# Two of seven panels of a propagation body summed from rows fetched by index instead of from the dense adjacency

## The reference

```
row, col = edge_index                      # src, dst
deg_row, deg_col = number of edges by row and by col, at least 1
w = rsqrt(deg_row[row] * deg_col[col])
def spmm(feat): return segment_sum(feat[col] * w[:, None], row, num_segments=n)
out = h
for _ in range(10):
    out = spmm(out) * 0.9 + h * 0.1
return out / theta
```

## Time and profile before

| | us |
|---|---|
| median of 2 runs | 3998.53 |
| lowest and highest | 3998.01, 3999.06 |
| the profiled execution, its span | 3998.4 |
| TensorE busy | 3854.9 |
| VectorE busy | 1769.7 |
| ScalarE busy | 1314.9 |
| GpSimd busy | 586.7 |

### The profile page before, as it was taken

The page is one execution under the profiler, slowest core; times in us unless marked ns, Lnnn a source line. Parts: engine busy times, 40 slices in busy tenths (PEclk is TensorE's granted clock), DMA queues, the critical chain, the costliest instruction groups (busy, mean ns, idle before and its releaser), DMA issues.

```text
span 3998.4 us, 124106 instructions
## 1 busy us (share of the span) xinstructions
PE 3854.9 (96%) x46183; PEld 3660.9 (92%) x46183; DVE 1769.7 (44%) x4393; ACT 1314.9 (33%) x3901; POOL 586.7 (15%) x714
## 2 busy tenths in 40 slices
PE   3889999999989999999999999999999998999999
PEld 2679999999956667999999999999999998999999
DVE  8999999999973324222222222222222222331111
ACT  1248888888871111222222122222222221111110
POOL 1016666666630000000000000000000000000000
PEclk9989999999989999999999999999999999999999
DMA  1039999889963333665665665656656665667775
GB/s 41 3 79 235 232 238 233 233 235 237 231 189 111 111 111 111 220 202 202 205 204 201 203 204 203 200 203 205 201 201 204 204 200 177 202 219 213 209 214 156
DMA packets 438001, 747.73 MB, mean 187 GB/s; under 512 B 197331, under 2 KB 330579, under 8 KB 437840
## 3 DMA queue, kind: packets, MB, share of 16 engines
q1 hardware_dynamic: 433346, 744.61, 61.1%
q10 hardware_dynamic: 4494, 0.77, 0.1%
HBM read 621.82 MB, written 83.32 MB: 176 GB/s over the span
## 4 chain that ended last, share of the span: by engine, by line
PE 91%; DVE 6%; ACT 1%; issue 1%; DMA 0%; ACTq 0%; DVEq 0%; SPq 0%; POOL 0%; POOLq 0%
PE sum L1795 49%; PE sum L1443 19%; PE pk L1182 10%; PE pr L1205 7%; PE pq L1194 3%; PE pc L1218 2%; DVE onerank L799 2%; PE l L475 1%; DVE bt L771 1%; DVE prodb L788 1%; DVE vals L781 1%; PE l L459 0%; DMA X<-in_x_dram 0%; DVE H L283 0%; PE sum L1622 0%
## 5 line engine op out<-in xcount | busy, mean ns | idle before, releaser
L1795 PE MATMUL sum<-u2b,ring 128*128 128x192 f16 x12005 | 994.1, 246 | 0.0
L1795 PEld LDWEIGHTS sum<-u2b,ring 128*128 128x128 fp8e4 x12005 | 993.1, 98 | 0.3
L1795 PE MATMUL sum<-y,ring 128*128 128x192 f16 x11662 | 962.9, 246 | 0.0
L1795 PEld LDWEIGHTS sum<-y,ring 128*128 128x128 fp8e4 x11662 | 962.2, 98 | 0.0
L1804 DVE TENSOR_TENSOR z<-lo,sum 128x96 f32<-128x96 f32 x441 | 112.2, 254 | 983.1 <-ACT lo L1819 982.8
L1182 PE MATMUL pk<-kv,hT 128*128 128x192 f16 x4900 | 485.6, 246 | 2.0 <-DVE hT L1074 2.0
L1443 PE MATMUL sum<-u,ring 128*128 128x385 f16 x2401 | 404.6, 329 | 12.4 <-ACT u L1585 12.4
L1182 PEld LDWEIGHTS pk<-kv,hT 128*128 128x128 f16 x4900 | 409.9, 99 | 2.4 <-DVE hT L1074 2.3
L1443 PEld LDWEIGHTS sum<-u,ring 128*128 128x128 fp8e4 x2401 | 236.0, 98 | 174.2 <-issue 13.6
L1264 ACT ACTIVATE kvs<-pk 128x384 f32<-128x384 f32 x735 | 301.0, 437 | 112.5 <-PE pk L1182 92.0
L1819 ACT ACTIVATE lo<-sum 128x96 f32<-128x96 f32 x441 | 110.1, 250 | 649.3 <-PE sum L1795 648.9
(11 more groups left out here) (254 smaller groups left out, 3363.3 us busy)
## 6 DMA issues: line engine op xcount, KB each, us to landing
ring<-adjacency_t SPq DMA_DIRECT2D x490, 800.0 KB, 4.3
ring<-adjacency SPq DMA_DIRECT2D x147, 896.0 KB, 4.9
rows<-slot_rows_d SPq DMA_DIRECT2D x249, 320.0 KB, 4.0
adjacency<-row SPq DMA_DIRECT2D x49, 800.0 KB, 4.4
adjacency_t<-col SPq DMA_DIRECT2D x49, 800.0 KB, 4.6
col<-row SPq DMA_TRANSPOSE x245, 4.1
out_dram<-X SPq DMA_DIRECT2D x6, 336.0 KB
slot_rows_d<-T SPq DMA_DIRECT2D x2, 240.0 KB
```

The source lines that it names most:

```text
L1795: m = pe.matmul(ps[r][:, 0:2 * D], w[:, t // 2, :, t % 2], n["this"][:, t, 0:2 * D], start=t == 0, stop=t == TILES - 1)
```

## The change

In steps 1 to 9 (nine of ten) panels 5 and 6 of each body are no longer read from the dense transpose. For each of the 25 lists of such a tile, GpSimd issues an indirect DMA (`gathers`): it takes 128 row numbers from a column of `k.index` and fetches those rows of 384 bytes from a copy of the table in memory (`u_d`) into `got[h][:, g, :]`. TensorE then sums 25 matmuls, with a 128x128 one-hot matrix of the list as weights (which slot belongs to which of the 128 nodes) and the fetched rows. There are two buffers `got`, and with two panels per body the first always serves panel 5 and the second panel 6: a panel's gathers wait until the same panel's matmuls of the body before are done. At a step's first body they also wait until the whole table is in memory (`k.u_out`); SyncE stores it body by body (`publish`), each store behind the loads of the next body.

The one-hot matrices of the 14 picked tiles are made once, by VectorE in the softmax layer (`one_hots`, seven ahead of the sums of block 0 and seven ahead of those of block 1, two buffers, each rewritten when its store has landed), and stored by GpSimd (`store`); SyncE loads them (400 KB) in place of those panels. The row numbers are computed once by GpSimd (`indices`) from the slots, which SyncE now copies to memory ahead of the attention's loads and GpSimd reads back with eight strided loads. The loops over bodies are written out inside the loop over pairs of steps on TensorE, SyncE and GpSimd. Several semaphores are used a second time instead of new ones.

```diff
+PICKS = 2
+PICKED = RING - PICKS
+PICKED_TILES = BODIES * PICKS
...
+    def sync():
+        sp.dma_start(k.slots_d, k.slots[:].rearrange("p i t g -> p (i t g)")).then_inc(k.slots_kept.sem, 16)
+        paired(sp, sync_step, SP_LAG)
...
+class Picked:
...
+    def indices(self):
...
+                pool.dma_start(planes[:, i, j * BODIES:(j + 1) * BODIES, :],
+                               of[:, i, PICKED + j:TILES:RING, :]).then_inc(k.slots_back.sem, 16)
...
+        pool.tensor_copy(k.index[:], part[1][:]).then_inc(k.listed.sem, 1)
+
+    def one_hots(self, j):
+        k, v = self.k, self.k.v
+        v.wait_ge(k.listed.sem, k.listed.at(2))
+        for b in range(j * BODIES, (j + 1) * BODIES):
+            if b >= 2:
+                v.wait_ge(k.hot_out[b % 2].sem, k.hot_out[b % 2].at(16 * (b // 2)))
+            v.tensor_tensor(self.hots[b % 2][:], under(k.count1[:], GROUPS), over(self.which[:, b, :], P),
+                            ALU.is_equal).then_inc(k.hot_built.sem, 1)
+
+    def store(self):
+        k, pool = self.k, self.k.pool
+        for b in range(PICKED_TILES):
+            pool.wait_ge(k.hot_built.sem, k.hot_built.at(b + 1))
+            pool.dma_start(k.hots_d[b, :, :], flat(self.hots[b % 2][:])).then_inc(k.hot_out[b % 2].sem, 16)
...
+            picked.one_hots(0)
             for i in range(BODIES):
+                if 1 <= i < PICKS:
+                    picked.one_hots(i)
                 v.wait_ge(k.agg.sem, k.agg.at(i))
...
         scalar(), vector(), scalar_sums(), tensor(), blocks.sync(early=1), first_loads()
+        picked.indices(), picked.store(), picked.end()
...
+    got = [k.buf(ctx, f"got{i}", [P, GROUPS, 2 * D], F16) for i in range(2)]
...
-            sp.dma_start(k.ring[r][:, 0:WIDE], k.t_d[RING * n["body"] + r, :, :]).then_inc(k.ring_in[r].sem, 16)
+            if r >= PICKED and n["turn"]:
+                sp.dma_start(k.ring[r][:, 0:GROUPS * P], k.hots_d[(r - PICKED) * BODIES + n["body"], :, :]).then_inc(k.ring_in[r].sem, 16)
+            else:
+                sp.dma_start(k.ring[r][:, 0:WIDE], k.t_d[RING * n["body"] + r, :, :]).then_inc(k.ring_in[r].sem, 16)
+
+    def publish(at, rows_of, h, b):
+
+        sp.wait_ge(k.u_ready.sem, k.u_ready.at(TILES + RING * at + RING))
+        k.settle(sp)
+        sp.dma_start(k.u_d[h][RING * b * P:RING * (b + 1) * P, :].rearrange("(t p) d -> p t d", p=P),
+                     rows_of[:, tiles_of(b), 0:2 * D]).then_inc(k.u_out[h].sem, 16)
+
+    def gathers(n):
+
+        b = n["body"]
+        if b == 0:
+            pool.wait_ge(k.u_out[n["table"]].sem, k.u_out[n["table"]].at(16 * BODIES * n["times"]))
+        for j in range(PICKS):
+            h, at = (PICKS * n["turn"][0] + j) % 2, j * BODIES + b
+            pool.wait_ge(k.done.sem, k.done.at(RING * (n["at"] - 2 // PICKS) + PICKED + j + 1))
+            k.settle(pool)
+            for g in range(GROUPS):
+                pool.indirect_dma_start(got[h][:, g, :], None, k.u_d[n["table"]], bass.IndirectOffsetOnAxis(
+                    ap=k.index[:, at, g:g + 1], axis=0)).then_inc(k.got[h].sem, 16)
...
+            if r >= PICKED and n["turn"]:
+                turn, seen = PICKS * n["turn"][0] + r - PICKED, PICKS * n["turn"][1]
+                pe.wait_ge(k.got[turn % 2].sem, k.got[turn % 2].at(16 * GROUPS * (seen + turn // 2 + 1)))
+                k.settle(pe)
+                w = k.ring[r][:, 0:GROUPS * P].bitcast(F8).rearrange("p (g e) -> p g e", e=P)
+                for g in range(GROUPS):
+                    m = pe.matmul(ps[r][:, 0:2 * D], w[:, g, :], got[turn % 2][:, g, :],
+                                  start=g == 0, stop=g == GROUPS - 1)
+                m.then_inc(k.done.sem, 1)
+                continue
```

More of the change, by code:

```diff
@@ L1850, in last_products, with sync, publish_before, gpsimd @@
                 unit.sums()
+    def sync():
+        for b in range(1, BODIES):
+            loads({"body": b, "at": b, "turn": None})
+            publish(b - 1, Ub, 1, b - 1)
+        with sp.Fori(0, last // 2) as s:
+            for n in pair(s):
+                loads(n)
+                publish_before(n)
+        for n in last_each():
+            loads(n)
+            if n["body"] == 0:
+                publish_before(n)
+    def publish_before(n):
+        h, b = n["table"], n["body"]
+        if b == 0:
+            publish(n["at"] - 1, n["this"], h, BODIES - 1)
+        else:
+            publish(n["at"] - 1, Ua if n["this"] is Ub else Ub, 1 - h, b - 1)
+    def gpsimd():
+        with pool.Fori(0, last // 2) as s:
+            for n in pair(s):
+                gathers(n)
+        for n in last_each():
+            gathers(n)
     def last_rows():
-        for n in last_numbers():
+        for n in last_each():
             b = n["body"]
@@ L1896, in last_copies @@
                 unit.root()
-    for n in numbers(sp):
-        loads(n)
-    for n in numbers(pe):
-        products(n)
+    sync(), tensor(), gpsimd()
     for n in numbers(v):
@@ L1905, in appnp_and_convolutions @@
         copies(n)
-    for n in last_numbers():
-        loads(n)
-    last_products(), last_rows(), last_copies()
+    last_rows(), last_copies()
     of_all = STEPS * BODIES
```

96 lines of the change are left out of this document (77 added, 19 removed).

## The result

The changed kernel takes 7825.85 us (median of 2 runs, 7824.85 to 7826.86) against 3998.53: 1.957 times as long (95% interval 1.953 to 1.961). The forecast was slower, and it was; but it said 5714 us with a range of 4600 to 6950, and the measured time lies 2112 us above the one and 876 above the other. The profiled execution has a span of 7821.8 us.

The account below looks back on a forecast made before the run. Matmuls bound the kernel before; GpSimd's gather issue would bind after. 3346 us of gathers plus 110 for steps, minus 1797, plus 54 preparation and 3 copy, gave +1716 on 3998.4: 5714 us, range 4600 to 6950.

Parts of the forecast that it names:

- TensorE's pace: Steps 1 to 9: matmuls bound the stretch before; 48 fewer per body save 4.0 us, 251 us over 63 bodies.
- The gather's price: GpSimd's issue of each gather: 1.06 us, ends 0.33 and 1.7; 3150 gathers make 3346 us in place of 1797.
- The overlap: Each body: panels 0 to 4 take 20.4 us beside the gathers, so the 50 issues alone set 53 us.
- The steps' gaps: Start of each step: first gather waits for the whole table, a 12.2 us chain; 110 us in sum.
- The transfers: DMA in each body: ring loads, gathers and publishing take 25 us, under the body's 53, so cost nothing.
- The preparation: Softmax layer: one-hot comparisons and indices make TensorE wait 31 and 23 us, 54 together, between 10 and 100.
- VectorE holds GpSimd back: Rival, in each body: descriptors stop for VectorE's two-input operations, 256 us more, 5970 us; chance 0.2, within the likeliest case.
- One gather at a time: Rival, GpSimd's queue: each gather waits for the landing before it, 1.7 us each, 7723 us; chance 0.05.
- Issue is hidden: Rival, GpSimd's queue: gathers under 0.52 us hide under TensorE, body 24.5 us, 3804 us; chance 0.03.
- the gather's spacing: Sign in the profile after, on GpSimd: one gather per about 1.06 us.
- the DMA share: Sign in the profile after, in the steps: DMA share near 0.45.
- TensorE's wait ahead of each picked panel ended by the gathers: Sign in the profile after, at panels 5 and 6: TensorE waits before each until its gathers end the wait.

Follow-up runs that it names:

- B: Series on chip 13, changed kernel with one edit each: plain loads by SyncE 4385 us; 64 rows a gather 7848; 32 bytes a row 7828; contiguous rows 7827.
- E: Series on chip 7 again: the changed kernel unedited, 7827 us; the changed kernel with TensorE's and GpSimd's code looped by turns, step 9 written out, 7825 us.
- F: Series on chip 10, one kernel: the changed kernel with 16-row gathers in odd steps, full gathers in even steps, 26 gathers a body in step 9; 7596 us.
- A: Series on chip 7, changed kernel with one edit each: no gathers 3808.8 us; plain loads by GpSimd 4183; 16 rows a gather 5994; TensorE's code looped 6310.
- C: Series on chip 4, edits of the changed kernel: 32 rows a gather 6060 us; 26 gathers a body, code written out 4430, TensorE's code looped 4433.
- D: Series on chip 15, changed kernel with one edit each: 26 gathers (first lists) 4433 us; 38 gathers 5357; 48 rows a gather 6110; GpSimd's code looped 6313.

## Why the forecast was wrong

The miss is 2112 us. By the forecast's terms, against the kernel with TensorE's loop (6307.7 us of span, held nowhere) and the changed kernel. The last column takes the gathers' price and the steps' gaps from the kernel at full pitch; what is left of its 5583 us is put down to the hold. The steps of the former, in the same columns as above:

```profile
1802.00:5875.00 4073.00, 1799.61 (x18679) 1737.25 (x18677) 406.47 (x1354) 347.62 (x1255) 2991.61 (x3150) 0.71 0.43 120
```

| term | forecast | full pitch | the change |
|---|---|---|---|
| 3150 gathers | 3346 | 3150 x 1.25 = 3938 | 3938 |
| steps' starts and ends | 110 | 4073 - 3938 = 135 | 135 |
| TensorE held beside them | 0 | 0 | 5583 - 4073 = 1510 |
| preparation, copy of the slots | 57 | 38 | 38 |

**TensorE's pace.** That the stretch was bound by matmuls before the change is right: without the gathers it gave what 48 matmuls a body are worth.

**The gather's price, mis-sized.** I took 1.06 us from the edge loads, since each reads its address from on-chip memory; it is 1.25 us, inside my ends of 0.33 and 1.7. This is worth 592 us. The likeness was luck: 0.53 us of the price are there with a plain load of as many rows too, the other 0.72 only with the indirect form, and of the whole only 0.10 go with 112 of the rows. The 0.62 us of the Trainium skill ("SBUF — State Buffer", section "SBUF: two separate sides") is the time of one GpSimd DMA alone and not of its issue; a plain issue takes 0.53 us here, a gather twice the page's figure.

**The overlap, the step that failed.** The prediction has it that "panels 0 to 4 (245 matmuls) take 20.4 us at the full clock, and panel 5 is done long before t = 53". In the changed kernel they take 85 us, because TensorE does not run at its pitch beside the gathers. I had looked for what could hold GpSimd back and never for what GpSimd could hold back. With it the body is 70.4 + 15.5 (the 168 matmuls left) + 3.0 (the first picked panel, which frees its buffer) = 88.9 us, and gathers and matmuls add where they should have overlapped. 1510 us, more than two thirds of the miss; without it the time would be 6310, inside the range. The fallen clock made this a little worse: 0.90 granted in the window of the fast stretch, 15.68 us for 168 matmuls, 93 ns each in place of 83.

**The steps' gaps.** The chain of 12.2 us was met to the tenth at full pitch, in part by luck: TensorE starts the last list 2.5 us after the last gather's end and not 1.7, and its 25 matmuls take 3.5 us and not 4.2 (the loop kernel at the end of step 1). In the changed kernel it is hidden: the first gather of step 2 comes 35 us after the last of step 1 instead of 26.7, but in these 8 us TensorE runs at full speed, 146 matmuls before it slows and not 38, so the body is not longer. TensorE and GpSimd at that place in the timeline:

```profile
2422.13 12.28 PE L1908 MATMUL sum<-y,ring 128*128 128x192 f16 x146
...
2429.46 0.94 POOL L1885 DMA_INDIRECT got<-u_rows_d,index  x1 [35.02 <-DMA u_rows_d<-y]
```

**The transfers.** Hidden, as said: a share of 0.32 in the steps at 88.6 us a body, where 25 us a body would be 0.28. Contiguous rows instead of scattered ones leave the time as it is (7827 and 7826 us), in kernels that the transfers do not bind.

**The preparation**, 54 us by my steps, shows up as 38 with the copy of the slots (step 0's first matmul at 1632.1 us, before at 1594.2). VectorE's comparisons and TensorE's two waits in the timeline:

```profile
1196.05 6.89 DVE L1533 TENSOR_TENSOR hots<-count,which 128x3200 uint8<-128x3200 bf16 x2
...
1224.49 18.25 PE L1456 MATMUL sum<-u,ring 128*128 128x385 f16 x98 [16.59 <-DVE ideg L1600]
...
1302.58 18.46 PE L1456 MATMUL sum<-u,ring 128*128 128x385 f16 x98 [17.06 <-DVE ideg L1600]
```

3.44 us a comparison, as taken; but the waits are 17 us each, not 31 and 23. The bringing back of the slots is eight issues in 7.8 us and 7.1 us more until they have landed, not 59: I had priced 128 short rows as if each 128 were an instruction. So the indices are ready at 1168.5 and not at 1211. And a stored one-hot panel of 400 KB lands in 2.7 us, not 4.3.

**The rivals.** "VectorE holds GpSimd back": the gathers stay at 1.25 us beside VectorE's operations (median 947 ns, mean 949 in the change and 950 at full pitch), so over 3150 gathers there is room for 6 to 9 us and not for 256; whatever stretches GpSimd's arithmetic in the earlier trace rows does not stretch gathers. "One gather at a time" came nearest in time (7723 us) and is wrong in substance: gathers are issued every 1.25 us and land 2.7 us later (the median of the two kernels with all 3150 gathers that are free). "Issue is hidden" would have needed 0.52 us; that is what a plain load costs, not a gather. Of the signs that I named, the gather's spacing, the step gap and the DMA share would have told the price apart from the rest; "TensorE's wait ahead of each picked panel ended by the gathers" is the one whose absence in the profile after, with no wait at L1898 at all, says that something else binds.

**What stays open.** What makes a kernel held, and by what path a gather stops TensorE, was not found. Held were the measured result, B, E and F, free A, C and D; chip 7 was in both kinds. The transfers of instructions take about 1 us for 16 KB in held and free kernels alike, and the slow stretch has only one or two of them, so it is not their volume. Whether a plain load from GpSimd would hold TensorE, and whether the unedited changed kernel is ever free, was not measured; the two kernels with all 3150 gathers and one looped stream say 6310 us for it, if it is.

One more thing in the traces parts the two kinds without exception. A gather reports its landing by 16 semaphore events. Of these events the trace of the kernel with TensorE's loop has 49,565 out of 50,400, and every free kernel's has 96 to 98%; the trace of the change has 7,599, and every held kernel's has 9 to 15%. The plain loads of SyncE in the held series B have all of theirs, and all matmuls are there in both kinds. So in held kernels most of the gathers' events, or the records of them, get lost. Whether this belongs to the cause of the hold or is a second effect of the same cause is open. Every time in this document has a recorded span beside it, so nothing here shows that the kernel would be held without the recording; the first experiment to make is the changed kernel timed with the recording off.

No version that fetches rows beats the kernel before. As an estimate from 1.25 us a gather, a body of 28.5 us has room for 22, and one picked panel needs 25 and saves 2.0 us.

## What to carry over

An indirect gather is here priced by the instruction, hardly by its rows: count them, multiply by the 1.25 us of GpSimd's time, and compare with what each one saves; 50 of them stood against 48 matmuls of 83 ns. When one engine's new work is to be hidden behind another's, the forecast must ask in both directions who can slow whom, and the range must hold the case that the two add rather than overlap. And before a condition is believed, the unedited kernel has to be run beside the edited ones, and one of the free ones again beside the held: for four series rows, number and loops all looked like causes, and two kernels that mixed these forms showed that none of them decides alone.

## What the hardware showed that was not expected

- An indirect DMA from GpSimd takes 0.95 us for 128 rows and 0.85 for 16, with 0.30 us between two; a plain one of the same 128 x 384 bytes takes 0.53 with nothing between. The gather of 128 rows lands in 2.7 us.
- In some series each indirect gather keeps TensorE back for 1.40 us: down to a matmul per 2.80 us in place of one per 83 ns, with no wait that the profile names and the DMA engines busy for 24%. In other series, once on the same chip, nothing of this is seen. The kernel before, without gathers, took 3998 to 4001 us (medians) in both. In the held kernels 85% and more of the gathers' landing events are missing from the trace, in the free ones 2 to 4%.
- SyncE issues 128-row loads in a dense run at 0.51 to 0.66 us each (25 in 12.65 and 25 in 16.56 us, in the kernel with SyncE's loads), where its 0.33 us for larger loads stood alone.
